# Moving the spreading of the first cross-attention's keys from VectorE to GpSimd in a two-layer perceiver kernel

## The reference, cut to what matters

```python
q = (queries @ Wq.T + bq).reshape(N, L, H, -1)      # N 64, L 32, H 16, 16 features a head
k = (keys @ Wk.T + bk).reshape(N, S, H, -1)
v = (values @ Wv.T + bv).reshape(N, S, H, -1)
sm = jnp.einsum('nlhd,nshd->nlhs', q, k) / math.sqrt(D)
sm = jnp.where(causal_mask[None, :, None, :], -jnp.inf, sm)
attn = jnp.einsum('nlhs,nshd->nlhd', jax.nn.softmax(sm, axis=-1), v)
return attn.reshape(N, L, H * D) @ Wo.T + bo
```

## Time and profile before

| what | value |
|---|---|
| median of 3 executions | 1524.1 us (1523.59 to 1524.49) |
| profiled execution, its own time | 1526.27 us |
| its span, first to last instruction | 1524.5 us |
| mean granted TensorE clock | 0.992 of full |
| busy: PE, DVE, ACT, POOL | 96%, 58%, 48%, 33% of the span |
| spreads of keys: X0 on DVE, A0 on POOL | 16 and 16 |

### The profile page before, as it was taken

How to read it: one execution, slowest core, us unless ns; L and a number is a source line. 1 busy time by engine, 2 the same in 40 slices (tenths; PEclk the granted TensorE clock), 3 DMA queues, 4 the chain that set the end, 5 groups by cost and what they waited for, 6 DMA issues and landing times.

```text
span 1524.5 us, 32958 instructions
## 1 busy us (share of the span) xinstructions
PE 1456.4 (96%) x12566; PEld 1119.0 (73%) x12566; DVE 881.9 (58%) x1909; ACT 730.7 (48%) x1799; POOL 508.1 (33%) x701
## 2 busy tenths in 40 slices
PE   6999998998999999999998998999999999999998
PEld 5877776446877777777775776588868877885887
DVE  5987997489646666666666888442234224323322
ACT  5887777488635555555554887322122212221211
POOL 2444552001026965976657888000000000000000
PEclk9999999999999999999999999999999999999999
DMA  8000000006222163146210000124404421441230
GB/s 309 22 7 3 1 1 22 0 0 181 69 114 77 47 229 107 49 165 234 55 48 2 2 1 2 49 101 154 146 0 151 153 96 49 146 160 47 101 141 14
DMA packets 60520, 124.13 MB, mean 81 GB/s; under 512 B 5008, under 2 KB 15760, under 8 KB 57872
## 3 DMA queue, kind: packets, MB, share of 16 engines
q1 hardware_dynamic: 60432, 122.94, 23.3%
HBM read 108.24 MB, written 14.68 MB: 81 GB/s over the span
## 4 chain that ended last, share of the span: by engine, by line
PE 77%; POOL 9%; DVE 7%; issue 4%; ACT 2%; DMA 1%; DVEq 0%; SPq 0%; POOLq 0%; ACTq 0%
PE ps L997 24%; PE ps L560 18%; PE ps L792 5%; PE ps L566 5%; PE ps L786 4%; PE ps L1048 4%; PE ps L814 3%; POOL R L2091 2%; POOL R L2073 2%; PE ps L802 2%; PE ps L825 2%; PE ps L909 2%; PE ps L764 1%; POOL R L2065 1%; PE ps L661 1%
## 5 line engine op out<-in xcount | busy, mean ns | idle before, releaser
L997 PE MATMUL ps<-R 128*128 128x256 f32 x1792 | 388.6, 380 | 3.4 <-DVE R L1915 3.4
L997 PEld LDWEIGHTS ps<-R 128*128 128x128 f32 x1792 | 340.5, 190 | 51.7 <-issue 6.4
L560 PE MATMUL ps<-R 128*128 128x128 f32 (+1 forms) x1344 | 306.0, 387 | 1.8 <-ACT R L1112 0.9
L560 PEld LDWEIGHTS ps<-R 128*128 128x128 f32 x1344 | 190.6, 195 | 109.7 <-issue 104.7
L2073 POOL TENSOR_TENSOR R<-R,c_inv 128x1024 f32<-128x1024 f32 x64 | 121.0, 1891 | 121.6 <-DVE c_inv L1801 121.6
L1320 ACT ACTIVATE R<-ps,c_nmx 128x257 f32<-128x257 f32 x256 | 118.0, 474 | 60.5 <-DVE c_nmx L1790 60.5
L1765 DVE COPY R<-ps 128x512 f32<-128x512 f32 x128 | 87.8, 686 | 77.2 <-PE ps L814 75.8
L792 PE MATMUL ps<-x_wv,R 128*128 128x256 f32 x512 | 131.3, 380 | 0.0
L2162 POOL TENSOR_SCALAR g_ve<-g_mv 128x4 f32<-128x4 f32 x4 | 0.9, 237 | 332.6 <-DVE g_mv L1864 332.5
L1312 ACT ACTIVATE R<-ps 128x512 f32<-128x512 f32 x64 | 38.2, 597 | 136.5 <-PE ps L792 136.5
L1392 ACT ACTIVATE R<-R,ffn_s 128x256 f32<-128x256 f32 x32 | 16.3, 508 | 167.4 <-DVE R L1922 167.4
(11 more groups left out here) (225 smaller groups left out, 2503.7 us busy)
## 6 DMA issues: line engine op xcount, KB each, us to landing
R<-quadrant_sums SPq DMA_DIRECT2D x32, 1024.0 KB, 6.8
R<-in_f_hq SPq DMA_DIRECT2D x32, 768.0 KB, 4.5
R<-in_ctxT SPq DMA_DIRECT2D x64, 257.0 KB, 2.7
R<-in_f_hq SPq DMA_DIRECT2D x8, 1024.0 KB, 8.8
quadrant_sums<-R SPq DMA_DIRECT2D x8, 1024.0 KB, 8.2
R<-in_ctxT SPq DMA_DIRECT2D x16, 256.0 KB, 3.6
k_ahead<-R SPq DMA_DIRECT2D x16, 256.0 KB, 3.7
R<-k_ahead SPq DMA_DIRECT2D x16, 256.0 KB, 3.1
```

The source lines that it names most:

```text
L560: r = mm(dst, w[:, ki, fo * P:(fo + 1) * P], src[:, ki, :], start=(ki == 0), stop=(ki == KI - 1))
L997: r = mm(ps[:, 4 * (g % 2) + bk, half * HALF:(half + 1) * HALF], f_wr[g % 3][:, w, ki * P:(ki + 1) * P], src[:, k, ki, :], start=(ki == 0) ...
```

## The change

The spread of X0's keys goes from DVE to POOL. d_keys is left for A1 alone, and X0's (7, d_keys) leaves DVE's list. b_keys, which A0 already uses, joins POOL's list for X0 at slot 16, two slots behind the bias. The instruction is the same one on the other engine. p_scores waits for k_spread in X0 too, and A0's and A1's waits count accordingly. On POOL a quarter of a round of X0 becomes: rsqrt L3, bias L2, keys L2.

```diff
             def p_scores(kind, l, n):
-                if kind == A0:
-                    pe.wait_ge(s["k_spread"], tile(n - BASE[A0], l))
+                if kind == A1:
+                    pe.wait_ge(s["k_masked"], tile(n - BASE[A1], l))
                 else:
-                    pe.wait_ge(s["k_masked"], tile(n if kind == X0 else n - NT, l))
+                    pe.wait_ge(s["k_spread"], tile(n, l))
...
             def d_keys(kind, l, i, n):
-                if kind == A1:
-                    ...
-                    r.then_inc(s["k_masked"], 1)
-                    return
-                dve.wait_ge(s["kT_copied"], KI * tile(n, l))
-                k = kT[l].rearrange("p (c k) -> p c k", k=L).unsqueeze(2).broadcast_to([P, 8, 4, L])
-                m = mask_hr[:, :].unsqueeze(1).unsqueeze(3).broadcast_to([P, 8, 4, L])
-                v.tensor_tensor(kbd[l][:, 0:8 * P].rearrange("p (c h k) -> p c h k", h=4, k=L), k, m, ALU.mult)\
-                    .then_inc(s["k_masked"], 1)
...
             run_lanes(dve, SLOTS0, [
-                attention(X0, [(0, d_norm), (7, d_keys), (8, d_turn_values), (10, d_mask), (10, d_max),
+                attention(X0, [(0, d_norm), (8, d_turn_values), (10, d_mask), (10, d_max),
...
             run_lanes(pool, SLOTS0, [
-                attention(X0, [(7, b_rsqrt), (14, b_bias)]),
+                attention(X0, [(7, b_rsqrt), (14, b_bias), (16, b_keys)]),
                 attention(A0, [(8, b_rsqrt), (12, b_bias), (17, b_keys)])])
```

More of the change, by code:

```diff
@@ L1438, in d_keys @@
             def d_keys(kind, l, i, n):
-                if kind == A1:
[L1441 to L1445, removed]
-                    r.then_inc(s["k_masked"], 1)
-                    return
-                dve.wait_ge(s["kT_copied"], KI * tile(n, l))
-                k = kT[l].rearrange("p (c k) -> p c k", k=L).unsqueeze(2).broadcast_to([P, 8, 4, L])
-                m = mask_hr[:, :].unsqueeze(1).unsqueeze(3).broadcast_to([P, 8, 4, L])
-                v.tensor_tensor(kbd[l][:, 0:8 * P].rearrange("p (c h k) -> p c h k", h=4, k=L), k, m, ALU.mult)\
-                    .then_inc(s["k_masked"], 1)
+                dve.wait_ge(s["qk_slots_ready"], tile(n - BASE[A1], l))
+                if isinstance(n, int) and n == BASE[A1]:
+                    dve.wait_ge(consts_made, 10)
+                for j in (0, 1):
+                    r = v.tensor_copy(key_block(l, j), key_rows(l, j))
+                r.then_inc(s["k_masked"], 1)
             def d_turn_values(kind, l, i, n):
```

## The result

The changed kernel takes 1543.26 us (median of 4, 1542.88 to 1546.19), the kernel before, on the same chip, 1524.3 us (median of 4). The ratio is 1.013, 95% interval 1.0118 to 1.0143: 19 us slower, where 21 were forecast. The changed kernel's profiled execution took 1543.27 us, with a span of 1541.5 us.

A forecast was written before the change was run, and what follows sets the result against it. PE was taken to bound X0 at 6.4 us a tile, a loop through POOL's keys afterwards at 8.0. 0.1 + 22.6 - 0.6 - 1.1 = +21.0 us on 1524.1 gives 1545.1 us, range 1539 to 1550, with A to 1555.

The forecast's parts named there:

- What bounds it: In X0's steady state PE alone sets the pace, 6.4 us a tile; the 18.6 us freed on DVE are worth nothing by themselves.
- POOL's last instruction for the norm: In X0 it falls from 0.98 to 0.19 us without DVE's keys beside it; otherwise 12 us more in all.
- The keys on POOL: 16 spreads added on POOL in X0, 1.89 us each, the median of the identical instruction in A0.
- The loop: X0's scores wait through DVE's norm, POOL's rsqrt, bias and keys: 8.01 us a tile, +22.6 us over 14 quarters.
- The first tile: X0's first keys start at 15.03 and end at 16.92 instead of 16.25; its scores come 0.1 us later.
- The passage: From X0 to A0: -0.6 us to the 16th tile's scores, then -1.1 us (bounds 0 and -1.9) from no clock fall.
- The rest: A0 and all behind it move as they are; PE's clock falls there may differ by 2 us either way.
- Rival A: PE's clock falls inside X0, 0.3 to 0.7 us a tile, 4.5 to 10.5 us more: 1550 to 1556; chance 0.19.
- B: Keys done in time, X0 stays PE-bound, gains at the change to A0 remain: 1520.5 to 1523 us; chance 0.04.
- C: The delay is paid once, not for every tile: +1.6 to +2.3 us, near 1526; chance 0.03.
- the low bound: Lower end of the whole kernel's forecast range, 1539 us, allowing for loop length, clock falls and the passage's clock gain.

The follow-up runs named there:

- e9: Kernel before, DVE's spread of X0's keys writing 128 instead of 1024 numbers a partition (scores not the reference's): 1522.5 us, ratio 0.9991.
- e6: Changed kernel with POOL's spread done twice for each tile of X0, same outputs: 1579.5 us, ratio 1.0372.
- e1: Changed kernel with POOL's keys of X0 ahead of the bias (slot 13, bias at 14): 1540.2 us, ratio 1.0099.
- e7: Changed kernel with POOL's keys of X0 ahead of the bias, at slots 14 and 15: 1533.7 us, ratio 1.0066.
- e10: Changed kernel, POOL's spread writing 128 instead of 1024 numbers a partition in X0, order and waits unchanged: 1524.3 us, ratio 0.9999.
- e3: Changed kernel with DVE's norm in X0 ahead of mask, maximum and shift, POOL's order unchanged: 1524.7 us, ratio 1.0003.
- e5: Changed kernel with PE's scores of X0 one slot later (9), behind turn and values: 1544.1 us, ratio 1.0132.
- e2: Changed kernel with POOL's keys of X0 ahead of the rsqrt too (slot 11): 1564.5 us, ratio 1.0255.
- e8: Changed kernel with DVE's norm ahead of the mask and PE's scores of X0 at slot 9: 1534.6 us, ratio 1.0073.

## Why the prediction was right

- **What bounds it.** PE set X0's pace before, nearly: beside e9's trace 0.12 us a tile were the collision of DVE and POOL. The prediction called the chain PE alone and the freed DVE time worth nothing by itself; the 15 us that e9 frees were worth about 2.
- **POOL's last instruction for the norm (L1981 before, L1974 after).** Forecast 0.19 us, measured 0.19 in X0 (78.50).
- **The keys on POOL.** Forecast 1.89 us, measured 1.89.
- **The loop.** Forecast 8.01 us, measured 8.00. Its parts fell where they were expected: mask 0.83 for 0.85, norm 2.89 for 2.90, rsqrt 3.84 for 3.85, keys 5.96 for 5.97. That it is closed is shown from both sides: made longer (e6) or shorter (e1, e7, e10) it gives back the length of the instruction that was added or taken from it, and cut (e3) it gives back 17 to 19 us; PE's order (e5) does nothing to it.
- **The first tile.** Forecast +0.1, measured +0.35; the keys started at 15.27 and not at 15.03, by 0.2 us of later start of everything in this execution.
- **The passage.** Forecast -0.6 to the 16th scores, measured 22.22 - 22.84 = -0.62. Forecast -1.1 for the clock, which had fallen there and was not to fall; measured 20.69 - 22.22 = -1.53. One point there was a near miss: DVE's constants were to fall into idle time. The first of them took 1.66 us behind POOL's spread, a collision that the prediction did not name, and the idle time was just long enough. The timeline of the changed kernel:

```profile
127.26 1.89 POOL L2002 TENSOR_TENSOR R<-R,mask_hr 128x1024 f32<-128x1024 f32 x1
...
128.03 1.66 DVE L1577 TENSOR_TENSOR posmask<-posmask,causal 128x512 f32<-128x512 f32 x1
129.30 0.67 PE L642 MATMUL ps<-R 64*32 64x128 f32 x32 [1.64 <-POOL R L2002]
...
130.16 0.69 DVE L1478 TENSOR_TENSOR R<-ps,causal 128x512 f32<-128x512 f32 x1
```

- **The rest.** The sum was +21.0, and up to A0's last tile the two traces differ by 20.9. Behind A0 the prediction said that all moves as it is, with 2 us either way for the clock. That bound was too narrow for the two traces: they give back 3.9 us. Compared matmul by matmul, the distance of the two traces stays constant over hundreds of us and changes at a few places. It shrinks by 2.7 us behind 250 us, by 1.5 between 818 and 842 and by 1.5 behind 951, places where the clock had fallen before and did not fall after; around 371 to 385 us, where one trace had a fall and then the other, it ends 1.4 us larger than at 365. Two smaller changes, +0.6 before 365 us and -0.35 behind 412, complete the 3.9. The medians, which are freer of this, differ by 19.0, 2.0 less than the sum, and the changed kernel's 1543.3 is 1.8 below the 1545.1 forecast; e5, whose pace is that of the changed kernel, is 20.1 above its kernel before. Why the falls come in one execution and not in another is open; no run here tells it.
- **Rival A, the clock falls inside X0,** came true in its cause and not in its price. In the changed kernel it fell four times in X0, each time behind one of PE's new gaps (1.36, 1.68, 1.72 and 1.68 us). The table by stretch for a tile with a fall:

```profile
89.41:97.44 8.03, 7.87 (x100) 6.67 (x101) 4.38 (x10) 5.36 (x15) 3.78 (x6) 0.79 0.06 16
```

The projection there took 4.26 us and not 2.94, and the scores still came 8.03 us after the last. The 1.6 us by which kT was early took it up. (By its busy time, 7.87 of 8.03 us, PE would look like the limit here; the pace is that of the tiles with 6.28.) I had priced such falls at 0.3 us or more a tile; the four together cost some 0.2. e2 is the counterpart, with 1.6 us for each.
- **Rivals B and C** are excluded by 15 steps of 8.0 us (7.92 to 8.13).
- **Slips in the bounds.** The terms named for the low bound (2.3, 2 and 0.8 us) give 1540.0 and not 1539, and the range with A ends at 1555 although A's prices go to 1556 and, with L1981 long, to 1557. B's gains of 0.6 to 1.7 us give 1523.5 and not 1523 at its upper end. None of this bears on the result.

## What to carry to other kernels

Before a step goes to the engine that looks idle, follow that engine's queue: what stands ahead of the moved step, what does that wait for, and does the answer lead back to the consumer of the step? If it does, the stage's pace is the length of this loop, whatever the busy shares say, and here it could be summed from the starts in one quarter of a trace to 0.1 us. To repair it, cut the loop at an edge that no data needs (here DVE's order of norm and mask); a step moved ahead of its input (e2), or to a place where the next loop starts (e8), only trades one loop for another.

## What the runs showed of the hardware

A fall of TensorE's clock has no fixed price. In the changed kernel and in e2 it fell behind idle times of similar length (1.68 and 1.48 us), and cost less than 0.1 us (a step of 8.03 against 8.00) where PE's projection had slack, and 1.6 where the projection was in the loop.

DVE and POOL held each other up in both directions: POOL's 0.19 us became 0.98 behind DVE's keys and 0.67 behind the shift (e3); DVE's 0.68 us operation on constants became 1.66 behind POOL's spread. In each pair the DVE instruction reads two operands in SBUF, and the later of the two ended with or after the earlier, 0.1 us or so sooner than a wait for all of the other and then its own time would give. The Trainium skill ("SBUF — State Buffer", section "Who interferes with whom") has this rule, and the three traces agree with it.
